# Attention scores laid out by destination in a two-layer graph network, with the missing edges of two block groups masked on VectorE

## The reference

```
h = relu(layernorm(x));  x = x + relu(h @ W_S.T + b_S + segment_sum(exp(-w) * (h[dst] @ W_N.T + b_N), src))
h = relu(layernorm(x))
q, k, v = h @ Wq + bq, h @ Wk + bk, h @ Wv + bv
logits = sum(q[dst] * k[src]) / sqrt(128)
alpha = softmax of logits over the edges of each dst
x = x + elu(segment_sum(alpha * v[src], dst) + h @ Ws + bs)
```

## Time and profile before

| | |
|---|---|
| median of 3 runs | 880.79 us (880.11 to 882.0) |
| the profiled execution | 879.39 us |
| its span | 877.6 us |
| TensorE busy | 770.2 us (88%) |
| VectorE busy | 725.2 us (83%) |
| ScalarE busy | 530.8 us (60%) |
| GpSimd busy | 255.2 us (29%) |
| attention stage | from 533 us to the end of the span |

### The profile page before, as it was taken

The page is one execution under the profiler, slowest core; times in us unless marked ns, Lnnn a source line. Parts: engine busy times, 40 slices in busy tenths (PEclk is TensorE's granted clock), DMA queues, the critical chain, the costliest instruction groups (busy, mean ns, idle before and its releaser), DMA issues.

```text
span 877.6 us, 23043 instructions
## 1 busy us (share of the span) xinstructions
PE 770.2 (88%) x8849; PEld 664.7 (76%) x8896; DVE 725.2 (83%) x883; ACT 530.8 (60%) x1034; POOL 255.2 (29%) x200
## 2 busy tenths in 40 slices
PE   0073899999999999999999777899999999999996
PEld 0052777777777777777776556799999999999996
DVE  6657999999999999999995635778878878878872
ACT  5954767676676766767665352455564565555554
POOL 5640000000000000000000320557657657656666
PEclk9996799999999999999999899899999999999999
DMA  9440113132131311313123602204334334324400
GB/s 231 140 131 2 77 78 150 75 131 94 75 149 75 140 84 84 140 75 149 75 93 132 262 38 75 76 2 156 112 122 155 112 121 155 127 106 155 144 18 11
DMA packets 17516, 94.96 MB, mean 108 GB/s; under 512 B 2594, under 2 KB 8844, under 8 KB 10956
## 3 DMA queue, kind: packets, MB, share of 16 engines
q1 hardware_dynamic: 14428, 89.18, 26.6%
q0 software_dynamic: 3056, 5.35, 2.5%
HBM read 50.31 MB, written 44.21 MB: 108 GB/s over the span
## 4 chain that ended last, share of the span: by engine, by line
PE 66%; DVE 16%; issue 10%; ACT 4%; POOL 1%; DMA 1%; DVEq 1%; POOLq 0%; SPq 0%; ACTq 0%
PE bank L1167 16%; PE bank L1177 14%; PE bank L1027 13%; DVE oh_key L872 6%; PE bank L1017 5%; PE bank L1089 5%; PE bank L1087 4%; PE bank L1164 3%; DVE kT L776 3%; PE bank L1131 2%; PE bank L1136 1%; ACT kT L510 1%; ACT qT L502 1%; DVE mx L948 1%; DVE oh_lo L869 1%
## 5 line engine op out<-in xcount | busy, mean ns | idle before, releaser
L456 POOL TENSOR_TENSOR sm<-sm,mbc 128x896 f32<-128x896 f32 (+1 forms) x100 | 186.0, 1892 | 47.2 <-ACT mbc L646 47.2
L1087 PE MATMUL bank<-oh_key,oh_lo 128*128 128x100 bf16 x1600 | 173.5, 210 | 12.7 <-DVE oh_key L872 11.4
L1027 PE MATMUL bank<-wsb,hvb 128*128 128x512 f32 (+1 forms) x350 | 165.2, 577 | 14.4 <-DVE kT L776 13.2
L1167 PE MATMUL bank<-qT,kT 128*128 (+1 forms) x1250 | 170.6, 278 | 3.6 <-DVEq L170 1.2
L1089 PE MATMUL bank<-oh_key,oh_lo 128*128 128x50 bf16 x3200 | 173.7, 188 | 0.0
L1167 PEld LDWEIGHTS bank<-qT,kT 128*128 128x128 f32 x1250 | 167.5, 195 | 5.0
L1087 PEld LDWEIGHTS bank<-oh_key,oh_lo 128*128 128x128 bf16 x1600 | 156.6, 98 | 18.7 <-DVE oh_key L872 11.6
L1089 PEld LDWEIGHTS bank<-oh_key,oh_lo 128*128 128x128 bf16 x3200 | 167.0, 98 | 1.1
L650 ACT ACTIVATE sm<-sm 128x896 f32<-128x896 f32 (+1 forms) x100 | 86.7, 867 | 108.9 <-POOL sm L456 108.9
L552 ACT COPY wsb<-bank 128x512 f32<-128x512 f32 (+1 forms) x175 | 87.9, 552 | 106.2 <-PE bank L1017 106.2
L1177 PE MATMUL bank<-vals,sm 128*128 128x129 f32 x1250 | 147.5, 274 | 0.2 <-ACT sm L650 0.2
(11 more groups left out here) (120 smaller groups left out, 725.4 us busy)
## 6 DMA issues: line engine op xcount, KB each, us to landing
gt<-gst SPq DMA_DIRECT2D x25, 1600.0 KB, 5.6
gl_sb<-gt SPq DMA_DIRECT2D x25, 1600.0 KB, 6.7
records<-rec SPq DMA_DIRECT2D x1, 1612.0 KB, 6.1
out<-res SPq DMA_DIRECT2D x24, 64.0 KB, 1.6
dst_i<-in_dst SPq DMA_DIRECT2D x1, 403.0 KB, 5.8
dstn_i<-in_dst_next SPq DMA_DIRECT2D x1, 403.0 KB, 6.8
src_i<-in_src SPq DMA_DIRECT2D x1, 403.0 KB, 7.3
w_in<-in_edge_weight SPq DMA_DIRECT2D x1, 403.0 KB, 8.0
```

The source lines that it names most:

```text
L456: pool.tensor_tensor(part, part, mbc[:, v % 2:v % 2 + 1, :].to_broadcast([P, n, P]), ALU.subtract).then_inc(sub_done, 1)
L1027: T.matmul(ps(6 + at)[:, 0:n], hvb[:, w, :], wsb[:, at, 0:n], start=True, stop=True).then_inc(l0_mm, 1)
L1087: T.matmul(cells, lo, oh_key[:, u, m, 0:2 * KEYS, i], start=True, stop=False, skip_group_check=True)
L1167: ins = T.matmul(score_bank(g)[:, j * P:(j + 1) * P], kT[:, (a + j) * P:(a + j + 1) * P], qT[:, bass.ds(t * P, P)], start=False, stop=True ...
```

## The change

The tile in `sm` is laid out by destination: column `d * 25 + h` holds destination d and source block h, where before it was `h * 128 + d`. The mask writes through that view, so its PSUM and `gl_sb` inputs stay contiguous and its output elements lie 25 elements apart. The maximum over h now reads `sm` in order. The subtraction and Exp of a group work on runs of 6 or 7 elements in each stretch of 25, and the value product loads its weights from every 25th element.

The logarithm is now taken of e times the count, so it is 1 for one edge and still about -41.6 for none. For groups 0 and 1 (13 of 25 blocks) TensorE has no mask matmuls any more, and its score products start the accumulation. In their place VectorE's new `lift` rewrites `gl_sb` in place as `min(gl * 2^60, gl)`, which leaves positive values and makes negative ones huge. It runs one tile ahead, for group 0 behind mask 0 and for group 1 behind mask 2. For groups 2 and 3 the mask matmuls stay, and `mark_absent` covers only these 1,536 columns, without its bias. The wait for `absent` moves to group 2.

```diff
+LIFT = 2
+LIFTED = SG[LIFT][0] * P
...
+        def by_dst(v, a, n):
+            return sm[:, v, :].rearrange("p (d h) -> p d h", h=NT)[:, :, a:a + n]
+
+        def by_source(v, a, n):
+            return sm[:, v, :].rearrange("p (d h) -> p h d", h=NT)[:, a:a + n, :]
...
-            pool.memset(steep_col[:], -STEEP).then_inc(s_init, 1)
...
-                    part = sm[:, v, a * P:(a + n) * P].rearrange("p (h d) -> p h d", d=P)
-                    pool.tensor_tensor(part, part, mbc[:, v % 2:v % 2 + 1, :].to_broadcast([P, n, P]),
+                    part = by_dst(v, a, n)
+                    pool.tensor_tensor(part, part, mbc[:, v % 2, :].unsqueeze(2).to_broadcast([P, P, n]),
...
-                    nc.scalar.activation(place, counts, ACT.Ln, bias=tiny_col[:, 0:1]).then_inc(evacs, 1)
+                    nc.scalar.activation(place, counts, ACT.Ln, bias=tiny_col[:, 0:1], scale=EULER).then_inc(evacs, 1)
...
-                nc.scalar.activation(absent[:, v % 2, :], gl_sb[:, v, :], ACT.Relu, bias=steep_col[:, 0:1],
-                                     scale=-STEEP).then_inc(absent_ready, 1)
+                nc.scalar.activation(absent[:, v % 2, LIFTED:], gl_sb[:, v, LIFTED:], ACT.Relu, scale=-STEEP).then_inc(absent_ready, 1)
...
-                        part = sm[:, w, a * P:(a + n) * P]
+                        part = by_dst(w, a, n)
...
-                V.tensor_tensor(sm[:, v, a * P:(a + n) * P], score_bank(g)[:, 0:n * P],
-                                gl_sb[:, v, a * P:(a + n) * P], ALU.add).then_inc(masked, 1)
+                if g < LIFT:
+                    dve.wait_ge(lifted, t * LIFT + g + 1)
+                V.tensor_tensor(by_source(v, a, n), score_bank(g)[:, 0:n * P].rearrange("p (h d) -> p h d", d=P),
+                                gl_sb[:, v, a * P:(a + n) * P].rearrange("p (h d) -> p h d", d=P), ALU.add).then_inc(masked, 1)
+
+            def lift(t, v, turn, g):
+
+                part = gl_sb[:, v, SG[g][0] * P:(SG[g][0] + SG[g][1]) * P]
+                if g == 0:
+                    dve.wait_ge(gl[v], turn * 16 + 16)
+                V.scalar_tensor_tensor(out=part, in0=part, scalar=STEEP, in1=part, op0=ALU.mult, op1=ALU.min).then_inc(lifted, 1)
...
+                if live(t + 1):
+                    lift(t + 1, (v + 1) % RING, turn + (v + 1) // RING, 0)
...
+                if live(t + 1):
+                    lift(t + 1, (v + 1) % RING, turn + (v + 1) // RING, 1)
...
-                    V.tensor_reduce(mx[:], sm[:, v, :].rearrange("p (h d) -> p d h", d=P), AX, ALU.max).then_inc(mx_ready, 1)
-
+                    V.tensor_reduce(mx[:], by_dst(v, 0, NT), AX, ALU.max).then_inc(mx_ready, 1)
+
+            for g in range(LIFT):
+                lift(0, 0, 0, g)
...
-                if g == 0:
+                if g == LIFT:
                     pe.wait_ge(absent_ready, t + 1)
                 pe.wait_ge(masked, t * NSG + g + 1)
                 for b, e in ((0, 4), (4, n)):
-                    T.matmul(score_bank(g)[:, b * P:e * P], minus_b[:], absent[:, v % 2, (a + b) * P:(a + e) * P], start=True,
-                             stop=False, skip_group_check=True)
+                    if g >= LIFT:
+                        T.matmul(score_bank(g)[:, b * P:e * P], minus_b[:], absent[:, v % 2, (a + b) * P:(a + e) * P],
+                                 start=True, stop=False, skip_group_check=True)
                     for j in range(b, e):
                         ins = T.matmul(score_bank(g)[:, j * P:(j + 1) * P], kT[:, (a + j) * P:(a + j + 1) * P],
-                                       qT[:, bass.ds(t * P, P)], start=False, stop=True, skip_group_check=True)
+                                       qT[:, bass.ds(t * P, P)], start=g < LIFT, stop=True, skip_group_check=True)
...
-                    ins = T.matmul(ps(4 + v % 2)[:, 0:D + 1], sm[:, v, h * P:(h + 1) * P], vals[:, h, :], start=h == 0,
+                    ins = T.matmul(ps(4 + v % 2)[:, 0:D + 1], by_dst(v, h, 1).rearrange("p d h -> p (d h)"), vals[:, h, :], start=h == 0,
```

More of the change, by code:

```diff
@@ L1 @@
+import math
 from contextlib import ExitStack
@@ L57 @@
 TINY = 2.0 ** -60
+EULER = math.e
 STEEP = 2.0 ** 60
@@ L127, in build_gnn @@
         tiny_col = sb(outer, "tiny_col", [P, 1])
-        steep_col = sb(outer, "steep_col", [P, 1])
         minus_b = sb(outer, "minus_b", [P, P], BF16)
@@ L275, in build_gnn @@
         gl = [sem(f"gl{k}") for k in range(RING)]
-        absent_ready = sem("absent_ready")
+        absent_ready, lifted = sem("absent_ready"), sem("lifted")
         s_ready, masked, mx_ready, mt_ready, m_ready, dg_ready, mb_ready, mbc_ready = (
@@ L488, in _ @@
             nc.scalar.activation(w_in[:], w_in[:], ACT.Exp, scale=-1.0).then_inc(s_ewx, 1)
-            act.wait_ge(s_init, 7)
+            act.wait_ge(s_init, 6)
             act.wait_ge(s_dst, 32)
@@ L562, in _ @@
                             nc.scalar.activation(f_g[:, 0, a * FH:(a + 1) * FH], ps(a)[:, 0:FH], ACT.Ln,
-                                                 bias=tiny_col[:, 0:1]).then_inc(fs_ev, 1)
+                                                 bias=tiny_col[:, 0:1], scale=EULER).then_inc(fs_ev, 1)
                             nc.scalar.copy(f_g[:, 1, a * FH:(a + 1) * FH], ps(2 + a)[:, 0:FH]).then_inc(fs_ev, 1)
@@ L699, in _ @@
                 V.tensor_copy(first_i[:, a:a + n], first[:, a:a + n]).then_inc(s_idx, 1)
-            dve.wait_ge(s_init, 7)
+            dve.wait_ge(s_init, 6)
             dve.wait_ge(s_ewx, 1)
@@ L1000, in _ @@
             pe.wait_ge(acc_ev, NPC)
-            pe.wait_ge(s_init, 7)
+            pe.wait_ge(s_init, 6)
             T.matmul(ps(6)[0:1, 0:1], badsum[:], ones[:, 0:1], start=True, stop=True).then_inc(s_badsum, 1)
```

## The result

The changed kernel takes 1,031.26 us (median, 1,029.9 to 1,032.99) beside 880.45 us for the kernel before on the same chip: a ratio of 1.171, 95% interval 1.1687 to 1.1734. The forecast was 871.2, so it had the wrong sign. The profiled execution has a span of 1,029.8 us.

A forecast was written before the change was run, and what follows sets the result against it. TensorE was taken to bound the attention stage, 12.995 us per step. Projections -6.1, ramp -1.5, steps -2.6 and tail +0.6 sum to -9.6 us: 869.8 for the profiled execution, 871.2 as a median, range 857 to 885.

The forecast's parts named there:

- Weights of the value product: Attention stage, TensorE: loading weights from `sm` 100 bytes apart costs zero extra, as line 1017's 194 against 191 ns.
- Weight loads pay for the step: Rival, value product: 50 loads per step cost 0.116 us more each, 5.8 us, 1,020 us in all; chance 0.02.
- writes 100 bytes apart are free: Rival, VectorE's masks: no write penalty, step 12.30 us, masks never late, -23.2 us, 857.6 us; chance 0.12.
- Reduction, 3.48 us: Attention stage, VectorE: the maximum over `sm`, made contiguous, takes 3.48 us, 2.36 us less.
- Masks of 768 at 1.52 us: Attention stage, VectorE: masks writing 100 bytes apart at 1.78 ns per element grow by 0.57 to 1.52 us.
- The step, 12.87 us: Attention stage, one tile: 12.30 us on TensorE plus 0.57 for the longer mask 1; 21 steps gain 2.6 us.
- Marks and projections, -6.1 us: Projection stage: two shorter `mark_absent` save 2.9 us, the recovered TensorE clock 3.2, together 6.1 us.
- Subtraction, 7.45 taken, 6.3 as a bound: Attention stage, GpSimd: the four subtractions stay at 7.45 us; lower bound 6.3 us.
- Ramp -1.5 and tail +0.6: Before steady state 1.5 us saved (0 to 3); at the end GpSimd's last two subtractions start 0.6 us later.
- The collision: Rival, attention stage: lift 0 waits for GpSimd's subtraction, step 13.2 us, +4.3 over 21 steps, 878.1 us; chance 0.18.
- The subtraction grows: Rival, GpSimd at line 456: four subtractions at 11.0 us make the step 13.7 us, 895 us in all; chance 0.12.
- Masks at 2.25 ns: Rival, VectorE's mask writes: at 2.25 ns VectorE becomes the bound at 13.9 us per step, 893 us; chance 0.06.

The follow-up runs named there:

- Experiment 1: The kernel before, with the value product reading weights from every 25th element of the old-layout `sm` and waiting for all four Exp: 1,035.52 us, ratio 1.178.
- experiments 3 and 4: The kernel before with its `wst` transposes as plain identity products, weights read from every 25th element, then contiguous: 1,078.37 and 930.15 us.
- experiment 2: The changed kernel, with the value product reading contiguous weights and each group waiting for all four Exp: 877.61 us, ratio 0.998.
- experiment 9: The changed kernel with `sm` laid out as before the change, masking of groups 0 and 1 still on VectorE: 861.85 us, ratio 0.9798.
- experiment 11: The changed kernel with source blocks 1 to 24 of `sm` in pairs (8-byte steps), block 0 alone, groups 0 and 1 lifted: 864.53 us, ratio 0.9811.

## Why the prediction was wrong, point by point

**The step that failed** is "Weights of the value product ... I take zero". The term measured 0.126 us per load, 6.3 us per step, 157 us in all. The rival "Weight loads pay for the step" named the place, the price (0.116 per load, 5.8 us per step) and the result (1,020 us; 25 steps of 5.8 on 871.2 make 1,016) within 1.5%, and got a chance of 0.02. Its price was borrowed from VectorE's reads, so that it came so near is partly luck. The error was in how the evidence was weighed. One row, of line 1017, agreed in step and type and differed in the mode of the product, while VectorE, ScalarE and GpSimd all paid for far-apart elements in the same table, and the rule on cachelines of the Trainium skill spoke against it too. A sentence in the rival "writes 100 bytes apart are free" built on the same row. Experiment 1 shows the cost of the order alone, experiments 3 and 4 that the mode makes the difference.

**The rest of the sum**, from experiment 2 (the change without this term, 877.6 us):

- *Reduction, 3.48 us:* it took 3.49. Right.
- *Masks of 768 at 1.52 us:* they took 1.62 to 1.64 us, (1.635 - 0.15) / 768 = 1.93 ns per element instead of 1.78. TensorE waits 0.82 us before group 3; the forecast was 0.7.
- *The step, 12.87 us:* it took 12.96 us, so the 21 steps gain 0.8 us and not 2.6.
- *Marks and projections, -6.1 us:* the marks are 1.47 us; from the start of the stage to the first scores it takes 37.7 us (489.21 to 526.91) instead of 43.8, -6.1, as forecast. In the changed kernel itself it takes 38.8, -5.0: there the first products of the stage ran at a lower clock (granted clock 0.87 over the stage, 0.95 in the experiment).
- *Subtraction, 7.45 taken, 6.3 as a bound:* it took 6.45. The lower bound was nearly right, so the four ended before lift 0 started, in this experiment by only 0.26 us.
- *Loop of the load, in the rival on the subtraction:* 672.34 - 666.09 less the mark of 2.96 is 3.3 us, not 3.4; it changes nothing.
- *Ramp -1.5 and tail +0.6:* they measured +1.7 and +4.6. The experiment's span, 876.7 us, is 8.7 above what the sum gives from the span before (877.6 - 9.6 = 868.0); 3.2 for the ramp, 4.0 for the tail and 21 x 0.09 = 1.9 for the step make 9.1, and 0.4 less lies before the stage. Most of the tail is the experiment's wait for all four Exp: TensorE idles 3.0 us before the last tile and then loads all 50 weights behind the last Exp (7.3 us at a granted clock of 0.78), where before 12 were left (1.4 us). How much of the ramp's error is mine was not separated.

**The rivals.** *Free writes* was wrong: the masks paid. *The collision* did not occur for lift 0 in the changed kernel (the subtraction ended before), but the mechanism is real. It shows there from the other side: line 475, ELU on GpSimd, takes 1.28 us while lift 0 runs from 707.45 to 708.54, and ends 0.31 us after it. In experiment 2, where the two do not meet, the same line takes 0.457. In experiment 9, where the four subtractions keep their 7.44 us, the overlap comes about, but only just: one lift 0 starts at 693.39, 0.28 us before the last of them ends, and takes 1.22 us instead of 1.09:

```profile
686.23 7.44 POOL L464 TENSOR_TENSOR sm<-sm,mbc 128x896 f32<-128x896 f32 x4 [2.02 <-ACT mbc L653]
...
693.39 1.22 DVE L928 SCALAR_TENSOR_TENSOR gl_sb<-gl_sb 128x896 f32<-128x896 f32 x1
```

The step there stays at 12.43 us, far from the rival's 13.2. The Trainium skill, SBUF — State Buffer, section "SBUF: two separate sides", calls this an exclusive lock between a VectorE instruction with two SBUF inputs and a GpSimd instruction that reads SBUF; lines 475, 989 and 947 agree. *The subtraction grows* had the wrong direction, 6.45 us instead of more than 7.45. *Masks at 2.25 ns* is refuted by 1.93 ns.

**Where the expected gain would have been.** The masking alone gives 2% (experiment 9, VectorE's masking of two groups and the shorter marks). The layout was to give back on the maximum what it took at the masks, and nearly did (2.35 us shorter; four masks 1.90 + 3 x 1.64 - 1.09 - 3 x 0.95 = 2.9 longer); the price came on an engine that the layout seemed not to touch.

## What to carry to other kernels

Before changing a layout, list every engine that reads or writes the tile, and count the 16-byte lines that each opens per element. In these runs float32 at 8 bytes is nearly free (TensorE 0.118 against 0.112 us per load, VectorE nothing), while TensorE's loads double at 16 and at 100 bytes (0.237 and 0.238 us), and its moving reads at 100 (0.236). Other types were not measured. A row is a price only for its own operation, mode included; where one row stands against all others of its table, give the others more than 2%. When two engines are both full, as in experiment 9, a gain on one alone is worth nothing, as experiment 11 showed.

## What the runs showed of the hardware that was not expected

- A transpose in transpose mode loads float32 weights 100 bytes apart at 0.113 us each; a plain product with the identity loads the same tile at 332 instead of 192 ns, a pitch of about 0.24, and twice per tile.
- The price of a far-apart load does not grow beyond 16 bytes: 0.237 us at 16, 0.238 at 100.
- TensorE's moving side pays the same at 100 bytes, 0.236 us per 128 columns.
- VectorE's float32 write 100 bytes apart costs 1.93 ns per element and its read 512 bytes apart 1.78; with two elements in each 16-byte line both cost 1.04, as when contiguous.
- GpSimd's subtraction is faster in the form with the repeated operand innermost: 6.45 us for the four instead of 7.44, and in pairs 6.54 and 0.46 for the single block. The order of the other operand changes with it, and the two were not separated.
- A small VectorE instruction with two SBUF inputs can have to wait out most of a GpSimd instruction: 1.53 us for 128 elements. A scalar operation on one tile (line 963) is held up too, 0.58 instead of 0.29 us.
